# Scales of two of a tile's four pairs of experts spread over the partitions by GpSimd instead of by a DMA

## What is computed

```python
def _L0_ffn_ref(hidden_states, ...):
    x = hidden_states.reshape(-1, H)
    scores = jax.nn.sigmoid(x @ gate_w.T)
    ...                      # two of four groups, then the eight best experts of them; weights sum to 2.5
    cw = zeros.at[tokens, topi].add(wsel)
    x_lat = x @ fc1_w.T
    h = relu2(jnp.einsum('tl,eil->eti', x_lat, w1))      # relu2 is the square of relu
    h = h * cw.T[:, :, None]
    y_lat = jnp.einsum('eti,eli->tl', h, w2)
    routed = y_lat @ fc2_w.T
    shared = relu2(x @ shared_up_w.T) @ shared_down_w.T
    return shared + routed
```

## Time and profile before

| | us |
|---|---|
| median of three executions | 433.8 |
| profiled execution | 432.69 |
| its span | 430.3 |
| PE busy (matmul) | 388.5 (90%) |
| DVE busy (VectorE) | 303.5 (71%) |
| ACT busy (ScalarE) | 258.9 (60%) |
| POOL busy (GpSimd) | 201.3 (47%) |
| mean granted clock of TensorE | 0.962 of 2.4 GHz |

### The profile page before, as it was taken

The page is one execution under the profiler, slowest core; times in us unless marked ns, Lnnn a source line. Parts: engine busy times, 40 slices in busy tenths (PEclk is TensorE's granted clock), DMA queues, the critical chain, the costliest instruction groups (busy, mean ns, idle before and its releaser), DMA issues. The chain is left out here.

```text
span 430.3 us, 7101 instructions
## 1 busy us (share of the span) xinstructions
PE 388.5 (90%) x2261; PEld 338.6 (79%) x2261; DVE 303.5 (71%) x602; ACT 258.9 (60%) x351; POOL 201.3 (47%) x154
## 2 busy tenths in 40 slices
PE   8689999999999979799999999999999999999620
PEld 8688889998898977578888888888878888898610
DVE  0058697598946655798888888888888888877300
ACT  2066163726566454677877878778777787876410
POOL 5000467677767100014645466554644455335562
PEclk9699999999999998999999999999999999999955
DMA  5993393923757278989999998889998889997432
GB/s 155 252 283 107 85 374 122 342 66 113 259 192 225 60 210 309 291 252 264 294 310 306 227 255 231 225 225 315 365 343 226 218 214 294 343 285 120 61 41 33
DMA packets 66826, 95.66 MB, mean 222 GB/s; under 512 B 19359, under 2 KB 48150, under 8 KB 66198
## 3 DMA queue, kind: packets, MB, share of 16 engines
q1 hardware_dynamic: 52786, 79.81, 57.5%
q0 software_dynamic: 13296, 15.08, 20.1%
q10 hardware_dynamic: 708, 0.32, 0.3%
HBM read 94.48 MB, written 30.18 MB: 290 GB/s over the span
## 5 line engine op out<-in xcount | busy, mean ns | idle before, releaser
L564 POOL DMA_INDIRECT out_x<-res,sid_sb x70 | 125.0, 1786 | 157.9 <-DMA out_x<-res,sid_sb 71.7
L1073 DVE TENSOR_TENSOR act_lo<-act_full,act_hi 128x1024 fp32r<-128x1024 f32 (+3 forms) x92 | 106.0, 1152 | 26.1 <-ACT act_full L913 15.8
L1335 DVE SCALAR_TENSOR_TENSOR scaled<-h_banks,cond_bd 128x1024 f32<-128x1024 f32 (+3 forms) x76 | 86.5, 1138 | 26.6 <-PE h_banks L733 23.2
L733 PE MATMUL h_banks<-xc_hi,w_ring 128*128 128x512 f32 (+1 forms) x272 | 87.1, 402 | 3.4 <-issue 1.5
L543 POOL DMA_INDIRECT rows_dram<-payload,slot_idx x64 | 69.3, 1083 | 42.5 <-DVE payload L1191 18.0
L911 ACT ACTIVATE act_hi<-scaled 128x1024 fp32r<-128x1024 f32 (+3 forms) x76 | 75.0, 987 | 3.7 <-DVE scaled L1335 3.3
L754 PE MATMUL y_banks<-act_hi,w_ring 128*128 128x512 f32 (+1 forms) x272 | 71.7, 386 | 3.9 <-ACT act_hi L911 3.9
L913 ACT ACTIVATE act_full<-scaled 128x1024 f32<-128x1024 f32 (+3 forms) x76 | 74.7, 983 | 0.0
L754 PEld LDWEIGHTS y_banks<-act_hi,w_ring 128*128 128x128 f32 x272 | 50.6, 190 | 14.4 <-ACT act_hi L911 4.0
L733 PEld LDWEIGHTS h_banks<-xc_hi,w_ring 128*128 128x128 f32 x272 | 46.2, 190 | 14.6 <-issue 5.7
L733 PE MATMUL h_banks<-xc_lo,w_ring 128*128 128x512 f32 (+1 forms) x136 | 52.4, 385 | 0.0
(11 more groups left out here) (183 smaller groups left out, 676.3 us busy)
## 6 DMA issues: line engine op xcount, KB each, us to landing
w_ring<-w_dram SPq DMA_DIRECT2D x68, 512.0 KB
cond_bd<-s_dram SPq DMA_DIRECT2D x64, 512.0 KB, 6.1
w_dram<-w_ring SPq DMA_DIRECT2D x8, 1024.0 KB, 7.9
x_in<-in_x SPq DMA_DIRECT2D x8, 512.0 KB, 6.9
res<-in_experts_raw SPq DMA_DIRECT2D x4, 1024.0 KB, 10.5
out_x<-x_in SPq DMA_DIRECT2D x8, 512.0 KB, 3.7
rows_sb<-rows_dram SPq DMA_DIRECT2D x16, 256.0 KB, 5.2
rows_dram<-in_pad_rows SPq DMA_DIRECT2D x5, 328.0 KB, 4.5
```

What stands on the lines that cost most here:

```text
L564: pool.indirect_dma_start(out, bass.IndirectOffsetOnAxis(ap=sid_sb[:, i % SID_RING, j, GROUP_SIZE:PER_GROUP], axis=0), res[:, i % 2, j * H ...
L733: last = pe.matmul(h_banks[:, s, m * BANK:m * BANK + SIZE[i]], w, v, start=n == 0, stop=n == 2)
L1073: dve.tensor_tensor(lo, full, hi.bitcast(f32), ALU.subtract).then_inc(act_lo_ready, 1)
L1335: dve.scalar_tensor_tensor(pair(scaled, i, u), h, 0.0, scale, ALU.max, ALU.mult).then_inc(scaled_ready, 1)
```

## The change

For pairs 0 and 1 nothing is changed. For pairs 2 and 3 (`SPREAD` = 2) of every tile the scales come in another way:

- SP loads the 4 x 512 values of both pairs as one row of 8 KB into one partition (`load_scale_rows`, two slots by i % 2, in the tile `payload`, which holds the token rows of stage one).
- GpSimd writes each pair's 2 x 512 values to all 128 partitions with `partition_broadcast` (`spread_scale`). For tile i it waits for `relu_and_scale(i - 1, u)`, as the DMA did, and for the row.
- The spreads of tiles 0 and 1 stand ahead of all adds, behind GpSimd's waits for all `store_shared` blocks. Those of tile i + 2 stand ahead of the adds of tile i.
- `relu_and_scale` waits for `scale_spread` in place of the DMA for these two pairs.

```diff
+BY_DMA = 2
+SPREAD = PAIRS - BY_DMA
...
+            def load_scale_rows(i):
+                if i >= 2:
+                    sp.wait_ge(scale_spread, SPREAD * (i - 1))
+                sp.wait_ge(s_stored[i % S_RING], (i // S_RING + 1) * DMA)
+                src = s_dram[i % S_RING, 2 * BY_DMA * SIZE[i]:2 * PAIRS * SIZE[i]].rearrange("(a t) -> a t", a=1)
+                sp.dma_start(scale_rows[:, i % 2, 0:2 * SPREAD * SIZE[i]], src)\
+                    .then_inc(scale_rows_loaded[i % 2], DMA)
...
-            for u in range(PAIRS):
+            load_scale_rows(0)
+            for u in range(BY_DMA):
                 load_scale(0, u)
...
             store_shared(7)
+            load_scale_rows(1)
...
-                        load_scale(i + 1, u)
+                        if u < BY_DMA:
+                            load_scale(i + 1, u)
...
+                    if u == 3 and i + 2 < X_TILES:
+                        load_scale_rows(i + 2)
...
             pool.wait_ge(out_zeroed, 2 * DMA)
+            def spread_scale(i, n):
+                u = BY_DMA + n
+                if i > 0:
+                    pool.wait_ge(scaled_ready, PAIRS * (i - 1) + u + 1)
+                pool.wait_ge(scale_rows_loaded[i % 2], (i // 2 + 1) * DMA)
+                pool.partition_broadcast(scale_ring[:, u, 0:2 * SIZE[i]],
+                                         scale_rows[:, i % 2, 2 * n * SIZE[i]:2 * (n + 1) * SIZE[i]]).then_inc(scale_spread, 1)
+
+            for i in range(2):
+                for n in range(SPREAD):
+                    spread_scale(i, n)
             for i in range(X_TILES):
+                if i + 2 < X_TILES:
+                    for n in range(SPREAD):
+                        spread_scale(i + 2, n)
                 pool.wait_ge(sid_loaded[i % SID_RING], (i // SID_RING + 1) * DMA)
...
-                dve.wait_ge(scale_loaded[u], (i + 1) * DMA)
+                if u < BY_DMA:
+                    dve.wait_ge(scale_loaded[u], (i + 1) * DMA)
+                else:
+                    dve.wait_ge(scale_spread, SPREAD * i + u - BY_DMA + 1)
```

6 lines of the change are left out of this document (5 added, 1 removed).

## The result

The changed kernel is slower. Its median is 442.5 us, against 433.73 us for the kernel before, run on the same chip. The ratio is 1.017, with a 95% interval from 1.009 to 1.026. The prediction was 429.6 us with a range of 426.0 to 437.5 us, so the time lies above the range and moved the other way than forecast. The interval leaves out 1, so the loss is real, but not whether it reaches 2%. One execution of the changed kernel, 447.82 us, was a slow one; the ratio is estimated without slow executions and so is not the quotient of the two medians. The profiled execution took 442.68 us, with a span of 440.8 us (before: 432.69 and 430.3 us). The last add begins at 433.87 us where it began at 423.33 us: 10.54 us later.

The account below looks back on a forecast made before the run. Two close bounds were taken: TensorE's pace in stage two and GpSimd's chain of adds, which sets the end. From the median, 433.8 us: -5.3 (landing) - 0.7 (weights) + 0.5 (VectorE) + 1.3 (start) = 429.6 us; range 426 to 437.5 us.

Parts of the forecast that it names:

- The start of stage two: Spread (0, 2) waits for the last `store_shared`, making scaling 3.2 us late: +1.3 us in all, ends 0 and +5.5 us.
- The relief: Ahead of the weights' stores two 512 KB transfers are gone, so the last store lands 3.0 us earlier, at 173.7 us.
- The slack: Tile 1's pair 0 waited for scales that now come sooner, so about 2.4 of the 3.2 us are absorbed.
- The clock: TensorE idles about 3 us at stage two's start, lowering its clock: +0.5 us, up to 1.7 us.
- The upper end that was kept: Most that stage two's start could cost: 0.8 + 3.0 (no relief) + 1.7 = +5.5 us.
- the start eats it: Rival: no relief ahead of the store and full clock loss, +5.5 in place of +1.3 us, 433.8 us; chance 0.18.
- The landing: GpSimd's adds land faster with emptier DMA queues: -5.3 us from tile 7 to 15, ends 0 and -8.3 us.
- The 13.3 us per tile: GpSimd's chain at DMA share 0.75, taken between 14.19 us at 0.84 and 12.46 us at 0.66; was 13.96 us.
- The spread on GpSimd: Each 1024-column spread takes about 1.1 us inside the wait for landing, costing the chain 0 up to about 2.1 us each.
- The hold of VectorE: Spreads stop VectorE's `act_lo` for part of 1.1 us, mostly taken up by idle time: +0.5 us, ends 0 and +3.2 us.
- the slower rival: Each spread stops VectorE at `act_lo` for its whole length, twice a tile: 445 us with 1.5 us spreads; chance 0.15.
- TensorE's wait for weights: TensorE's one DMA wait in the middle stretch, for weights, goes away: -0.7 us.

Follow-up runs that it names:

- run with one broadcast: The kernel before plus one partition broadcast of 8 columns, issued by GpSimd after the scatter and ahead of the first add: 440.58 us, ratio 1.021.
- run with the broadcast first: The kernel before plus one 8-column broadcast at the very start of GpSimd's program, ahead of the first select: 433.23 us, ratio 1.001.
- early spreads: The changed kernel with the spreads of tiles 0 and 1 moved ahead of GpSimd's waits for stores and zeroed rows: 436.72 us, ratio 1.007.
- run with small weights: The changed kernel with moved selects and spreads moved ahead of the stores' waits, stage two's new weight loads cut to 8 columns: 424.56 us, ratio 0.981.
- spreads alone: The kernel before, all loads kept, plus 38 spreads from and into a spare part of `payload`: 442.9 us, ratio 1.021.

## Why the prediction was wrong, by its own steps

**The missing term: +6.3 us.** The sum began at stage two. This step failed by leaving a term out: the new kind of instruction was priced by its duration alone. The order of instructions has one bare instruction of GpSimd ahead of the first select, in both kernels, and a second one ahead of the first spread, in the changed kernel only. In the trace of before the first select waited 0.25 us; with the second bare instruction in the program it waited 8.68 us. The run with one broadcast shows the whole price, and the run with the broadcast first shows that the order makes it. That the price is one of loading code is the likeliest account, not a seen one.

**The start of stage two: +7.25 us in place of +1.3.** This is the step that failed most within the sum. The place and the mechanism were right: `relu_and_scale(0, 2)` waited for its spread, and the spread for the last store. Four sizes were wrong. (1) The relief: the store was to land 3.0 us earlier, as two loads were gone from ahead of the weights' stores. Less the 6.29 us of the late start, SP issued it at 171.75 us in place of 172.31 us, 0.6 us earlier. SP waited 176.02 - 165.09 = 10.9 us from the issue of the weights' stores, against 170.28 - 157.72 = 12.6 us before; this row of SP's timeline of the kernel before gives the issue:

```profile
157.72 1.50 SPq L368 DMA_DIRECT2D w_dram<-w_ring  x2
```

So shorter queues took 1.6 us off, and the stores' own issue came 1.1 us later within the program. (2) The store landed in 4.5 us, near the 4.4 us taken, but the spread began only 182.97 - 178.04 = 4.9 us after the issue, and it took 1.3 in place of 1.1 us. Together pair 2 was scaled 6.35 us late (184.36 - 6.29 - 171.72), in place of 3.2. (3) The slack: 2.4 us of the delay were to be absorbed, as tile 1 waits for its scales anyway. Half of that came. Tile 1's pair 0 was scaled at 191.49 us, 191.49 - 6.29 - 180.02 = 5.18 us late, so 1.2 us were absorbed; it no longer waited for its scales but for TensorE:

```profile
191.49 1.22 DVE L1372 SCALAR_TENSOR_TENSOR scaled<-h_banks,cond_bd 128x1024 f32<-128x1024 f32 x1 [1.31 <-PE h_banks L767]
```

(4) The clock: +0.5 us were taken, 1.7 us the most. Behind the 6.10 us of idle time the clock granted to TensorE was 0.53 from 187 to 194 us, 1.2 GHz for nearly all of that time; by this row it cost up to 0.47 x 7 = 3.3 us, an estimate. From tile 1's pair 0 to tile 0's copy another 2.07 us were lost, behind products that TensorE made late and in part at this clock, and so 7.25 us went through.

```profile
187.00:194.00 7.00, 6.45 (x16) 4.49 (x17) 5.53 (x5) 2.63 (x3) 2.17 (x2) 0.53 0.06 9
```

(The row is a window of the changed kernel, columns as above.) The upper end that was kept, +5.5 us, assumed no relief but the 2.4 us of slack whole; it was too low mainly by the slack that did not come, 1.2 us. The rival "the start eats it" had named this, at 433.8 us. The early spreads show that it is the wait: without it the same stretch takes 22.18 us.

**The landing: right in kind, under half in size.** The chain was to gain 5.3 us, all of it from tile 7 to tile 15. Tile 15's lag fell by 2.37 us in this pair of executions, but from the first add of tile 7 to that of tile 15 the chain took 110.45 us in place of 111.71 us: 1.26 us. The rest was there before tile 7, where the prediction put nothing: tile 7's lag was 298.31 - 296.66 - 0.60 = 1.05 us in place of 286.93 - 283.49 - 0.60 = 2.84 us. A chain that has nearly caught up with TensorE has no more to gain. Over the runs, the lag of tile 15 is 8.87 to 10.05 us in the six kernels with all loads of scales (mean 9.30) and 4.78 to 7.17 us in the five kernels with two spreads that load their weights and scales whole (mean 6.41): 2.9 us. The 13.3 us per tile were read from a line through two windows, and a third one of the same trace does not lie on it: at share 0.90 a tile took 13.34 us, less than the 14.19 us at 0.84. This is its row, of the kernel before:

```profile
344.39:357.73 13.34, 13.23 (x66) 10.92 (x65) 11.39 (x16) 10.32 (x15) 6.44 (x4) 1.00 0.90 213
```

The main mistake was one DMA share for all tiles. The mean did fall to 0.80 in the second half, not to 0.75, but the tiles differ. Three windows of the changed kernel, from the first add of tile 7 to that of tile 15, then tiles 8 and 10:

```profile
298.31:408.76 110.45, 109.41 (x565) 92.11 (x563) 95.67 (x115) 84.89 (x120) 73.25 (x48) 1.00 0.80 202
314.27:328.66 14.39, 14.28 (x72) 11.76 (x71) 12.21 (x15) 11.39 (x17) 10.39 (x7) 1.00 1.06 298
339.09:352.03 12.94, 12.84 (x65) 10.60 (x64) 11.67 (x15) 9.97 (x15) 8.68 (x7) 1.00 0.68 145
```

Tile 8's stretch moved 14.39 x 298 = 4.3 MB, tile 10's 12.94 x 145 = 1.9 MB. The difference is about four loads of 512 KB, those of a group's weights, which move only where the ring does not hold the next tile's group yet (`cond=need_of[i]`). Where they don't, the lag is gone within two or three tiles: 0.9 us at tile 12. Where they do, it comes back: at tiles 8 and 9, and at 13 to 15, and that last time there is no tile left to recover in. A queue that is less full on the mean sets the end only as far as it is less full in the last two or three tiles. The run with small weights shows that the weights do it: without them the lag does not come back at tiles 8, 9, 13 and 14.

**The spread on GpSimd: right.** 0 was taken for the chain. A spread of 1024 columns takes 1.30 us where it begins beside no two-input operation of VectorE, and 1.73 us where it begins while `act_lo` runs (at 213.78 us, `act_lo` from 213.12 to 214.35 us), within the bounds of 0.88 and 6.3 us and near the 1.1 us taken. This row of the changed kernel gives all 38:

```profile
L581 POOL PARTITION_BROADCAST cond_bd<-payload x38 | 58.8, 1616 | 49.4 <-DMA payload<-s_dram 33.2 <-DVE scaled L1372 16.1
```

**The hold of VectorE: right, and so the slower rival was not what made it slower.** `act_lo` ran 112.5 us in place of 106.0 us, 6.5 us in all, by these rows of the changed kernel and of the kernel before:

```profile
L1107 DVE TENSOR_TENSOR act_lo<-act_full,act_hi 128x1024 fp32r<-128x1024 f32 (+3 forms) x92 | 112.5, 1222 | 21.6 <-ACT act_full L947 11.2 <-ACT act_full L928 10.2
...
L1073 DVE TENSOR_TENSOR act_lo<-act_full,act_hi 128x1024 fp32r<-128x1024 f32 (+3 forms) x92 | 106.0, 1152 | 26.1 <-ACT act_full L913 15.8 <-ACT act_full L894 10.2
```

One that meets a spread is this pair (VectorE, GpSimd):

```profile
203.24 1.81 DVE L1107 TENSOR_TENSOR act_lo<-act_full,act_hi 128x1024 fp32r<-128x1024 f32 x1
```

```profile
202.81 1.30 POOL L581 PARTITION_BROADCAST cond_bd<-payload  x1 [0.66 <-DVE scaled L1372]
```

It takes 1.81 us in place of 1.22 and ends 0.94 us after the spread. By the rule of the Trainium skill that the prediction named ("SBUF — State Buffer", "Who interferes with whom") it should stand still until the spread ends; the rows come close to that, since it would then have ended 1.22 us after. But TensorE's pace is 13.19 us per tile, not slower than 13.26, with and without the relief (13.20 us with the spreads alone): VectorE's idle time takes it up. The +0.5 us were 0. TensorE's wait for weights (0.7 us) is gone, and the pace gave 1.05 us in this pair; over the table's runs 13.20 to 13.26 us with all loads of scales stand against 13.17 to 13.19 us with two, so on the mean 0.6 us of it holds.

**The sum again**, by the steps: -2.4 (lag) - 1.05 (pace, with the weights) + 0 (VectorE) + 7.25 (start of stage two) + 6.3 (start of the program) + 0.4 (the tail) = +10.5 us, in place of -4.2 us. Had the first spreads stood ahead of the stores' wait and a broadcast at the program's start, the forecast would have been near: 427.63 us, and 425.78 us with the selects moved in place of the broadcast, against 429.6 us. That nearness is luck in part: in the first of these two the start of stage two gained 1.5 us where +1.3 us were forecast, and the lag fell to 7.17 us where 4 us were, and the two misses cancel.

## What to carry to other kernels

A new kind of GpSimd instruction can have a price at the other end of the program, here 8.6 to 8.8 us of idle time: look at which kind comes first and which later, and see whether the later kind, put first once, takes the wait away, as it did here. Put the first use of a new step ahead of every wait that it does not itself need; a step that takes over from a DMA inherits the waits of the queue that it is put into. Where a shared resource is relieved, ask what it does in the last tiles, not on the mean.
